# Shared-expert chunks of a fused attention and expert block: the first two moved into the last attention group, the last two among the first expert tiles

## The reference

```python
def _swiglu(x, wg, wu, wd):
    return jax.nn.silu(x @ wg) * (x @ wu) @ wd
...
probs = jax.nn.softmax(xn @ gate_w.T, axis=-1)     # xn: layernorm of x with scale and bias
tk_probs, tk_idx = jax.lax.top_k(probs, TOP_K)     # 2 of 8 experts for each token
...
out = _swiglu(xf, sWg, sWu, sWd)                   # the shared expert, every token
for e in range(NUM_EXPERTS):
    out = out + w[:, e:e + 1] * _swiglu(xf, Wg[e], Wu[e], Wd[e])
```

## Time and profile before

| what | us |
|---|---|
| median of 3 runs (lowest, highest) | 803.59 (802.44, 805.21) |
| the profiled execution | 806.09 |
| its span, first to last instruction | 804.4 |
| busy in the span: PE, DVE, ACT, POOL | 667.4, 610.2, 505.1, 323.1 |
| mean granted TensorE clock, as a share of 2.4 GHz | 0.952 |

### The profile page before, as it was taken

The page is one execution under the profiler, slowest core; times in us unless marked ns, Lnnn a source line. Parts: engine busy times, 40 slices in busy tenths (PEclk is TensorE's granted clock), DMA queues, the critical chain, the costliest instruction groups (busy, mean ns, idle before and its releaser), DMA issues.

```text
span 804.4 us, 17228 instructions
## 1 busy us (share of the span) xinstructions
PE 667.4 (83%) x6081; PEld 323.6 (40%) x6112; DVE 610.2 (76%) x1262; ACT 505.1 (63%) x1055; POOL 323.1 (40%) x437
## 2 busy tenths in 40 slices
PE   5786368999989889899879899888888889799961
PEld 2332022333334324234324334323246777587741
DVE  5989758888887897987897987987526476455667
ACT  3655036787767878687778677778656544344653
POOL 3675111122212233172533163533453137776642
PEclk9999569999999999999999999999799999899995
DMA  6446451120131131240230321202603112363534
GB/s 155 137 152 171 120 164 21 50 50 21 33 76 31 22 76 47 57 107 15 61 76 29 75 70 47 65 29 63 202 27 107 40 51 81 83 191 98 158 105 129
DMA packets 88785, 66.18 MB, mean 82 GB/s; under 512 B 27728, under 2 KB 75249, under 8 KB 88703
## 3 DMA queue, kind: packets, MB, share of 16 engines
q1 hardware_dynamic: 80076, 54.24, 26.5%
q0 software_dynamic: 4352, 8.99, 3.4%
q10 hardware_dynamic: 4274, 1.87, 0.9%
HBM read 38.11 MB, written 24.46 MB: 78 GB/s over the span
## 4 chain that ended last, share of the span: by engine, by line
PE 45%; DVE 22%; ACT 7%; issue 6%; POOL 3%; DMA 3%; SPq 2%; POOLq 0%; ACTq 0%; DVEq 0%
DVE block_max L343 13%; PE ps L1998 11%; PE ps L2025 8%; PE ps L328 5%; PE ps L2105 3%; ACT expT L1453 3%; PE ps L335 3%; PE ps L1975 2%; SPq L1194 2%; PE ps L2086 2%; PE ps L2094 1%; PE ps L2063 1%; DMA q_space<-negT 1%; PE ps L2088 1%; PE ps L2087 1%
## 5 line engine op out<-in xcount | busy, mean ns | idle before, releaser
L1453 ACT ACTIVATE expT<-ps 128x512 f32<-128x512 f32 (+1 forms) x640 | 325.3, 556 | 134.8 <-PE ps L2025 129.7
L343 DVE TENSOR_REDUCE block_max<-ps 128x8 f32<-128x1024 f32 x288 | 340.0, 1218 | 57.6 <-PE ps L328 38.7
L1998 PE MATMUL ps<-expT,vr 128*9 128x256 f32 (+1 forms) x2560 | 181.8, 366 | 16.5 <-ACT x_in L1413 14.9
L2025 PE MATMUL ps<-q_space,k_space 64*128 64x512 bf16 (+3 forms) x768 | 165.8, 338 | 10.0 <-DMA q_space<-negT 6.6
L1370 POOL TENSOR_SCALAR_AFFINE_SELECT expT<-expT 128x512 f32<-128x512 f32 x128 | 83.0, 661 | 195.5 <-ACT expT L1453 195.4
L328 PE MATMUL ps<-k_space,q_space 64*128 64x128 bf16 (+3 forms) x1152 | 132.0, 280 | 34.7 <-DVE block_max L343 24.4
L2025 PEld LDWEIGHTS ps<-q_space,k_space 64*128 64x128 bf16 x768 | 46.0, 94 | 153.2 <-ACT expT L1453 102.4
L1385 POOL DMA_INDIRECT expert_rows<-expT,tile_to x72 | 70.0, 973 | 59.1 <-ACT expT L1488 40.4
L1998 PEld LDWEIGHTS ps<-expT,vr 128*9 128x9 f32 x2560 | 42.1, 89 | 98.9 <-issue 47.1
L328 PEld LDWEIGHTS ps<-k_space,q_space 64*128 64x128 bf16 x1152 | 49.5, 95 | 74.0 <-DVE block_max L343 58.3
L1323 POOL TENSOR_SCALAR negs<-block_max 128x32 bf16<-128x32 f32 x16 | 4.7, 296 | 133.1 <-DVE block_max L1575 133.1
(11 more groups left out here) (235 smaller groups left out, 927.4 us busy)
## 6 DMA issues: line engine op xcount, KB each, us to landing
expT<-sorted_rows SPq DMA_DIRECT2D x72, 65.0 KB, 1.9
expT<-expert_rows SPq DMA_DIRECT2D x14, 256.0 KB, 5.1
q_parts<-parts SPq DMA_DIRECT2D x24, 128.0 KB, 2.3
...
```

Of the source, the lines that this page charges most:

```text
L343: nc.vector.reduce_max(bm[:, g % 2, 2 * f:2 * f + 2, at:at + 4], ps[:, 2 * odd:2 * odd + 2].rearrange("p h (n k) -> p h n k", k=P), AX_X). ...
L1453: act.activation(expT[:, (NS * g + s) % PTN, hh, 0:width], ps[:, B_S + n % S_RING, 0:width], ACT.Exp, scale=SCALE).then_inc(exp_ok, 1)
L1998: last = nc.tensor.matmul(ps[32 * hh:32 * hh + VW, B_O, at:at + n], vr[:, g % RING, kt, hh * VW:(hh + 1) * VW], expT[:, (NS * g + s) % PTN ...
L2025: last = nc.tensor.matmul(ps[:, B_S + n % S_RING, col:col + m], head_rows(kr, g, hh, slice(kt * P, (kt + 1) * P)), head_rows(qr, g, hh, sl ...
```

## The change

- The `half` units of chunks 0 and 1 and their down products become items of PE's list in group 15, at slots 5, 8, 18, 20, 26 and 33 (`AHEAD`); the second part of each follows one slot later. Silu there is `z * (tanh(z/2) + 1) / 2`: ACT takes tanh, and DVE two `scalar_tensor_tensor` of 128x512 instead of one multiplication (`gated_ahead`, two slots after the item). DVE, not ACT, keeps the down products.
- Units start at 4 (`FIRST_U`); `chain` keeps its place counted from there. Chunks 6 and 7 go behind tiles 4, 5 and 6, 7; tile 35 is the last unit. `turn_rows` of tiles 0 and 1 now stands in the third and fourth unit after attention. It waited also for `normed[0]`; that wait goes to `turn_h`. The projection of the last chunk uses another bank.
- The weights are split slice by slice: high parts on ACT (slots 8 and 18), low parts on POOL (steps 4 and 6) of groups 1, 2, 3, 8 and 12 (`SPLIT`).
- On SP's queue the fill of the spare rows moves to group 1, the down weights to group 13, four of the six `xf` chunks to group 14.
- POOL scatters the fourth sequence four at a time behind the sends of tiles 5 to 8. The output steps that stood in units 47 to 51 follow the last unit.

```diff
     for c in range(CHUNKS):
-        if c in (4, 5):
+        if c >= 4:
             seq += [("tile", 2 * (c - 4) + i, 0) for i in range(2)]
-        if c == CHUNKS - 2:
-            seq += [("tile", q, 0) for q in range(4, NP)]
         seq += [("half", c, i) for i in range(2)]
-    return seq
+    return seq + [("tile", q, 0) for q in range(8, NP)]
 
 
 UNITS = units()
+AHEAD_C = 2
+FIRST_U = 2 * AHEAD_C
+AHEAD = {5: ("half", 0, 0), 8: ("half", 0, 1), 18: ("down", 0, 0), 20: ("half", 1, 0), 26: ("half", 1, 1), 33: ("down", 1, 0)}
+SPLIT = {1: (0, 1), 2: (2, 3), 3: (4, 5), 8: (6, 7), 12: (8,)}
 LEFT_P = NP - 8
 OUT_FIRST = 4
...
     plan = [[("sum", 0)], [("stats", 0)], [("shift", 0), ("sum", 1)], [("stats", 1)], [("shift", 1), ("sum", 2), ("row", 0)],
-            [("stats", 2), ("sum", 3), ("stats", 3)], [("shift", 2), ("shift", 3), ("row", 1)], [],
-            [("row", 2)], [("row", 3)]]
+            [("stats", 2)]]
     return {first + i: parts for i, parts in enumerate(plan)}
 
 
 OUT_PARTS = out_parts()
-NORM_AT = {UNITS.index(("tile", LEFT_P + 2, 0)) + at: c for c, at in enumerate((3, 5, 7, 8))}
+NORM_AT = {UNITS.index(("tile", LEFT_P + 2, 0)) + at: c for c, at in enumerate((3, 5))}
 LAST_TILE = UNITS.index(("tile", NP - 1, 0))
...
+            if g == G - 1 and slot in AHEAD:
+                order.append((g, slot, *AHEAD[slot], None))
...
+            tanhs = k_words[:, 10 * CT:12 * CT].rearrange("p (i n) -> p i n", i=2)
...
-            B_ROWS, B_PROJ = (B_Y, B_HT), (B_ONE, B_XT)
+            B_ROWS, B_PROJ = (B_Y, B_HT), (B_ONE, B_HT)
...
+                def get_turned(c):
+                    sp.wait_ge(xf_out[c % 2], DMA * (c // 2 + 1))
+                    sp.dma_start(xf_in[:, c], xf_d[c]).then_inc(xf_back[c > 1], DMA)
+
                 def side(g, slot):
                     q, r = side_pair(g), g % NG
+                    if (g, slot) == (1, 24):
+                        sp.wait_ge(empty_ok, 2)
+                        sp.dma_start(xs_d[SPARE:].rearrange("(n p) w -> p n w", p=P),
+                                     empty[:].unsqueeze(1).to_broadcast([P, NE, XW])).then_inc(padded, DMA)
+                    if g == G - 3 and slot in (8, 26):
+                        rows = slice(P * (slot > 8), P * (slot > 8) + P)
+                        sp.wait_ge(lo_ok, NE + 1)
+                        sp.dma_start(w_gu[:, 0:NE, rows], wd_d[:, rows, :].rearrange("e k h -> k e h")).then_inc(down_in, DMA)
+                        sp.dma_start(w_gu[:, NE, rows], swd_d[rows, :]).then_inc(down_in, DMA)
+                    if g == G - 2 and slot in (12, 16, 20, 24):
+                        sp.wait_ge(pv_done, NS * (G - 2))
+                        get_turned((slot - 12) // 4)
                     if q < 0:
...
-                sp.wait_ge(lo_ok, 2)
-                for i in range(2):
-                    rows = slice(P * i, P * (i + 1))
-                    sp.dma_start(w_gu[:, 0:NE, rows], wd_d[:, rows, :].rearrange("e k h -> k e h")).then_inc(down_in, DMA)
-                    sp.dma_start(w_gu[:, NE, rows], swd_d[rows, :]).then_inc(down_in, DMA)
...
-                for c in range(CHUNKS - 2):
-                    sp.wait_ge(xf_out[c % 2], DMA * (c // 2 + 1))
-                    sp.dma_start(xf_in[:, c], xf_d[c]).then_inc(xf_back[c > 1], DMA)
-                sp.wait_ge(empty_ok, 2)
-                sp.dma_start(xs_d[SPARE:].rearrange("(n p) w -> p n w", p=P),
-                             empty[:].unsqueeze(1).to_broadcast([P, NE, XW])).then_inc(padded, DMA)
+                for c in range(CHUNKS - 4, CHUNKS - 2):
+                    get_turned(c)
...
+                def low_weights(e):
+                    pool.wait_ge(hi_ok, e + 1)
+                    nc.gpsimd.tensor_tensor(w_lo[:, e], w_gu[:, e], w_hi[:, e], ALU.subtract).then_inc(lo_ok, 1)
+
                 def side(g, s):
                     q, r = side_pair(g), g % NG
+                    for at, e in zip((4, 6), SPLIT.get(g, ())):
+                        if s == at:
+                            low_weights(e)
...
-                first, each_time = 4, 3
+                first, each_time = 5, 4
                 for q in range(NP):
                     send_rows(q)
                     lo = each_time * (q - first)
                     if 0 <= lo < 2 * PAIR_T:
                         rows_sent(LAST, lo, min(each_time, 2 * PAIR_T - lo))
-                    if q in (LEFT_P + 2, LEFT_P + 4):
+                    if q in (LEFT_P + 2, LEFT_P + 4, LEFT_P + 6):
                         out_root((q - LEFT_P - 2) // 2)
 
-                for c in range(2, CHUNKS):
+                for c in range(3, CHUNKS):
                     out_root(c)
...
+                def high_weights(e):
+                    if e == 0:
+                        act.wait_ge(late_in, DMA * LATE)
+                    act.activation(w_hi[:, e], w_gu[:, e], ACT.Copy).then_inc(hi_ok, 1)
+
+                def tanh(p, c, i):
+                    act.wait_ge(sh_gate, 2 * c + i + 1)
+                    wait(act, sh_hu, 2 * (c - 1) + i + 1)
+                    act.activation(tanhs[:, i], ps[:, bank_of(p)], ACT.Tanh, scale=0.5).then_inc(sh_silu, 1)
+
                 def side(g, slot):
                     q, r = side_pair(g), g % NG
+                    for at, e in zip((8, 18), SPLIT.get(g, ())):
+                        if slot == at:
+                            high_weights(e)
...
+                    if g == G - 1:
+                        for p, _, at, kind, c, i, _ in of_group(g):
+                            if kind == "half" and slot == at + 1:
+                                tanh(p, c, i)
                     if (g, slot) == (G - 1, 36):
-                        x_high(0)
+                        x_high(AHEAD_C)
 
...
+                def rows_ahead(c):
+                    dve.wait_ge(xf_back[0], DMA * 2)
+                    v.tensor_copy(x_hi[:, c % 2], xf_in[:, c]).then_inc(x_hi_ok, 1)
+                    x_low(c)
+
+                def gated_ahead(p, c, i):
+                    dve.wait_ge(sh_up, 2 * c + i + 1)
+                    dve.wait_ge(sh_silu, 2 * c + i + 1)
+                    v.scalar_tensor_tensor(tanhs[:, i], tanhs[:, i], 1.0, ps[:, bank_of(p)], ALU.add, ALU.mult).then_inc(sh_mid, 1)
+                    dve.wait_ge(sh_mid, 2 * c + i + 1)
+                    wait(dve, sh_down, c)
+                    v.scalar_tensor_tensor(hu[:, i], tanhs[:, i], 0.5, ps[:, bank_of(p) + 1], ALU.mult, ALU.mult).then_inc(sh_hu, 1)
+
+                def keep_ahead(p, c):
+                    dve.wait_ge(sh_down, c + 1)
+                    v.tensor_copy(shared[:, c].rearrange("p t e -> p (t e)"), ps[:, bank_of(p)]).then_inc(sh_kept, 1)
...
+                    if g == G - 2 and slot in (36, 38):
+                        rows_ahead((slot - 36) // 2)
+                    if g == G - 1:
+                        for p, _, there, kind, c, i, _ in of_group(g):
+                            if kind == "half" and slot == there + 2:
+                                gated_ahead(p, c, i)
+                            if kind == "down" and slot == there + 3:
+                                keep_ahead(p, c)
...
-                    if g == G - 1:
-
-                        dve.wait_ge(late_in, DMA * LATE)
-                        for i, es in enumerate((slice(0, 5), slice(5, NE + 1))):
-                            v.tensor_copy(w_hi[:, es], w_gu[:, es]).then_inc(hi_ok, 1)
-                            dve.wait_ge(hi_ok, i + 1)
-                            v.tensor_tensor(w_lo[:, es], w_gu[:, es], w_hi[:, es], ALU.subtract).then_inc(lo_ok, 1)
...
+                out_shift(2)
+                out_sum(3)
+                out_stats(3)
+                out_row(1)
+                out_shift(3)
+                out_row(2)
+                out_row(3)
...
+                def up_ahead(p, c, i):
+                    three_passes(ps[:, bank_of(p) + 1], slice(INTER + P * i, INTER + P * (i + 1)), c).then_inc(sh_up, 1)
+
+                def down_ahead(p, c, part):
+                    if part == 0:
+                        pe.wait_ge(down_in, DMA * 4)
+                        pe.wait_ge(sh_hu, 2 * c + 2)
+                    for t in range(2 * part, 2 * part + 2):
+                        for i in range(2):
+                            last = nc.tensor.matmul(ps[:, bank_of(p), t * P:(t + 1) * P], hu[:, i, t * P:(t + 1) * P],
+                                                    w_gu[:, NE, P * i:P * (i + 1)], start=i == 0, stop=i == 1)
+                    if part == 1:
+                        last.then_inc(sh_down, 1)
 
...
+                    elif kind == "half":
+                        pe.wait_ge(x_lo_ok, g + 1)
+                        pe.wait_ge(lo_ok, NE + 1)
+                        three_passes(ps[:, bank_of(p)], slice(P * which, P * (which + 1)), g).then_inc(sh_gate, 1)
+                    elif kind == "down":
+                        down_ahead(p, g, 0)
...
```

(11 more changed lines are left out.)

55 lines of the change are left out of this document (29 added, 26 removed).

## The result

The change made the kernel slower by half a per cent: 808.14 us (median of 12 runs, 805.86 to 813.02) against 803.67 for the kernel before (12 runs). The ratio is 1.0054, 95% interval 1.0036 to 1.0071. I had said 800.0 us, 795.5 to 806.0, and faster with 0.58; I had taken 0.3% as what can be told from no change. The profiled execution took 810.2 us, its span is 808.5, its mean granted clock 0.941.

The account below looks back on a forecast made before the run. PE, then DVE, was taken to hold the chain, with PE at half clock in the last group. Terms 0.9 + 3.8 + 2.7 - 7.0 - 4.0 = -3.6 gave 802.5 us profiled, median 800.0, range 795.5 to 806.0.

Parts of the forecast that it names:

- Weights split, +0.9: Groups with split weights: ACT's nine added copies, 5.7 us, almost hidden, a sixth showing; bounds 0 and 5.7 us.
- Last group, +3.8: Last attention group: moved halves and down products delay `ranks` and add PE work; group ends at 596.4 instead of 592.6 us.
- unit count: 0: Units between attention and tile 35: 12 half and 36 tile units before and after, so gains there come from waits.
- half of the low clock: Last group: PE's clock expected low for 6.8 us, half of the 13.6 us seen before.
- Rival, clock does not fall in the last group: Last group without low clock ends 3.3 us earlier than forecast: 796.7 us; chance 0.14.
- Rows of tile 0, +2.7: Third unit: PE waits 4.3 us for rows, less 1.6 us of mask wait saved; bounds 0 and +6.
- Middle tiles, -7.0: Middle tiles: POOL scatters earlier, so 7.0 of 7.6 us lost to waits for rows go; bounds 0 and -7.6.
- End, -4.0: Last send to DVE's first sum of chunk 4: 6.7 us instead of 10.7, not under 5.6; bounds 0 and -5.1.

Follow-up runs that it names:

- before: The kernel before the change, unaltered, first profile: profiled execution 806.09 us, span 804.4; median 803.67 us.
- after: The change as made, against the kernel before, first profile: profiled execution 810.2 us, span 808.5; median 808.14 us, ratio 1.0054.
- second pair: Both kernels, unaltered, profiled once more: before 805.35 us (span 799.0), changed 806.08 us (span 803.5).
- before_again: The kernel before the change, unaltered, profiled once more: 805.35 us, ratio 1.0005.
- after_again: The change, unaltered, profiled once more against the kernel before: 806.08 us, ratio 1.0022.
- slot22_2: The change with ACT's second weights copy of a group in slot 22 instead of 18, repeat run: 805.60 us, ratio 1.0016 to the kernel before.
- both_2: The change with ACT's second copy in slot 22 and chunk 4 before tiles 0 and 1: 799.71 us, ratio 0.9951 to the kernel before.
- one_chunk_end: The change with chunk 7 and its output steps behind tile 35 again: 812.32 us, ratio 1.0093 to the kernel before.
- scatter_3_2: The change with ACT's second copy in slot 22 and POOL's scatters three at a time as before: 806.41 us, ratio 1.0035 to the kernel before.

## Why the prediction was wrong

- **Weights split, +0.9.** Mis-sized. I took a sixth of ACT's 5.7 us as an average over everything. It was no average: 0.5 us in each of four groups, 2.0 in all, all of it from the copy that stands in front of the one copy PE waits for. The row for it was there before (the wait for `x_in`, 0.7 us), and I had not looked at what stands ahead of each copy.
- **Last group, +3.8, and "unit count: 0" as the gain behind it.** This is the step that failed. In the profiled pair the term reads +4.5 from the last placing (+4.2 from the group's first block), near what I said, but by luck: I had forecast half of the low clock, and there was none, so by my sum the group should have grown by 0.5. The error of 3.7 us is above all the price of a slot at full clock. I halved PE's busy time of the slots at low clock (12.88 us for fourteen, so 0.46 each). Measured: `ranks` to first unit 23.5 us, less two down products of 4.4 and two halves of 3.6, is 15.5 us for 27 slots, 0.57 each, where my prices make 11.4: 4.1 too little. The moved work behind `ranks` took 8.0 us for 7.1, 0.9 more. `ranks` itself came 1.6 us later and not 3.0, 1.3 less. PE's instructions are not twice as long at 1.2 GHz: a product of 0.62 us takes 1.04, a block of scores of 0.39 takes 0.60. From one product, with two blocks behind it, to the next it is 1.52 us in the low stretch of `before` and 0.87 in `after`:

```profile
583.58 1.04 PE L1998 MATMUL ps<-expT,vr 128*9 128x256 f32 x8
585.10 1.04 PE L1998 MATMUL ps<-expT,vr 128*9 128x256 f32 x8
```

```profile
590.03 0.62 PE L2086 MATMUL ps<-expT,vr 128*9 128x256 f32 x8
590.90 0.62 PE L2086 MATMUL ps<-expT,vr 128*9 128x256 f32 x8
```

So PE bounds the group behind `ranks` at either clock (busy 19.6 of 21.0 us in `before`, 15.4 of 17.1 in `before_again`, 23.1 of 23.5 in `after`), and the room that I saw in it was that of one execution. In the second pair, with 6.8 us of low clock in the group before the change and 3.4 after it, the moved work costs 9.4 us of the stage.

- **Rival, clock does not fall in the last group.** It happened in the profiled execution, and the group was longer all the same: by my sum the time should have been 796.7. In `after_again` the clock is low for 3.4 us, ahead of `ranks`.
- **No term: falls of the clock elsewhere.** 4.8 us of the profiled pair's difference (3.4 in group 7, 0.7 in group 8, 0.7 in group 11) are falls at waits that the kernel before has too. Of the second pair's difference they are 0.5. They blur a single profile by more than the changes that one wants to read in it.
- **Rows of tile 0, +2.7.** The wait is right, 4.29 us in the third unit (4.3 forecast), with the mask wait gone but for 0.2. Its price is mis-sized: the sum had no term for the low clock behind it, and with every pair of tiles one chunk later the median falls by 5.9 us on one chip (`slot22_2` to `both_2`). With that and the copy in slot 22, the kernel is about as fast as I had forecast for the change.
- **Middle tiles, -7.0.** The wait went, as forecast, but mostly for another reason than POOL's order, as `one_chunk_end` and `scatter_3_2` show. First unit to last send gave -2.7 where rows and middle together should have given -4.3; the low clock behind the wait for tile 0 (1.7 us on the down product alone) would make up the difference.
- **End, -4.0.** -5.3: the first sum comes 5.5 us after the last send, a little under my lower end of 5.6. The output steps of chunk 3 fit into the time of the sends' landing, for which I had charged 1.1 us.

With the numbers of the profiled pair the sum is +2.0 for the split, +4.5 for the last group, -2.7 for the units, -5.3 for the end, +4.8 for the falls elsewhere and 0.8 for the rest: +4.1, where I had -3.6. More than half of this miss is the falls. With the numbers of the second pair it is +2.0, +9.4, -2.2, -5.1 and 0.4 for the rest: +4.5, and there the group alone is 5.6 us off.
